# First attention of a two-layer block: the scaling of a pair's values on GpSimd instead of VectorE, its output product moved to the end of the step

## The reference, cut to what matters

```
x = x + attn0(layernorm(x))       # 16 heads of 64; q, k, v through 128x64 and 64x1024 weights
    scores = q @ k.T / 8          # 1024 x 1024 for each head and batch
    out = softmax(scores) @ v ; out @ fco_w + fco_b
x = x + ffn0(layernorm(x))        # 8 experts
    probs = softmax(logits); the two largest, divided by their sum, are the gates
    out = sum of gate * (silu(h1) * h2) @ down
x = x + attn1(layernorm(x)); x = x + ffn1(layernorm(x))
```

## Time and profile before

| | us |
|---|---|
| median of 3 runs | 1484.37 |
| lowest, highest run | 1483.67, 1501.54 |
| profiled execution: time | 1491.57 |
| its span | 1489.8 |
| its mean granted clock of TensorE | 0.967 |

### The profile page before, as it was taken

The page is one execution under the profiler, slowest core; times in us unless marked ns, Lnnn a source line. Parts: engine busy times, 40 slices in busy tenths (PEclk is TensorE's granted clock), DMA queues, the critical chain, the costliest instruction groups (busy, mean ns, idle before and its releaser), DMA issues. The chain is left out here.

```text
span 1489.8 us, 18635 instructions
## 1 busy us (share of the span) xinstructions
PE 1384.4 (93%) x6322; PEld 786.9 (53%) x6322; DVE 985.4 (66%) x1675; ACT 816.6 (55%) x1236; POOL 869.5 (58%) x685
## 2 busy tenths in 40 slices
PE   6699999999999999999988976899999997999998
PEld 5344445444544444444456733445444445687776
DVE  5677777777777767567546667676666724566665
ACT  4244444444444445444345444466776565787776
POOL 0298787778887867687654505455565332344443
PEclk9699999999999999999999997899999998999999
DMA  3110111111101111000040006011111106000000
GB/s 106 33 44 16 57 59 57 45 58 59 58 26 47 58 44 44 15 16 15 26 158 1 1 0 100 7 24 29 30 29 29 30 2 270 1 1 8 8 8 8
DMA packets 32586, 60.59 MB, mean 41 GB/s; under 512 B 9499, under 2 KB 17084, under 8 KB 32348
## 3 DMA queue, kind: packets, MB, share of 16 engines
q1 hardware_dynamic: 32492, 59.40, 14.4%
HBM read 35.13 MB, written 13.89 MB: 33 GB/s over the span
## 5 line engine op out<-in xcount | busy, mean ns | idle before, releaser
L628 POOL TENSOR_TENSOR psum_k<-psum_k,prob 128x1024 f32<-128x1024 f32 x186 | 464.3, 2519 | 78.7 <-ACT prob L680 78.7
L680 ACT ACTIVATE prob<-pair 128x1024 f32<-128x1024 f32 x256 | 249.4, 1025 | 388.7 <-PE pair L931 388.7
L738 DVE TENSOR_REDUCE mx<-pair 128x2 f32<-128x1024 f32 x256 | 303.9, 1221 | 83.5 <-PE pair L864 83.0
L903 PE MATMUL pv<-prob,c_all 128*64 128x512 f32 x1024 | 247.7, 605 | 0.0
L1928 DVE CUSTOM_DVE_ANT_0 l_banks<-l_banks,causal 128x128 f32<-128x128 f32 (+7 forms) x256 | 189.5, 783 | 74.3 <-PE l_banks L1966 73.3
L930 PE MATMUL pair<-qq,ak 128*128 128x512 f32 x512 | 221.5, 433 | 3.5 <-issue 2.4
L1836 ACT ACTIVATE l_prob<-l_banks 128x1024 f32<-128x1024 f32 (+7 forms) x256 | 155.2, 654 | 110.8 <-PE l_banks L1985 110.1
L931 PE MATMUL pair<-q,kb 128*128 128x512 f32 x512 | 202.3, 395 | 0.0
L2144 POOL TENSOR_TENSOR silu_rest_t<-silu_t,silu_lead_t 128x512 fp32r<-128x512 f32 x74 | 96.4, 1304 | 144.4 <-ACT silu_lead_t L2341 144.4
L1890 POOL TENSOR_SCALAR_AFFINE_SELECT l_prob<-l_prob 128x128 f32<-128x128 f32 x256 | 72.3, 295 | 146.2 <-ACT l_prob L1836 144.6
L930 PEld LDWEIGHTS pair<-qq,ak 128*128 128x128 f32 x512 | 97.0, 190 | 72.7 <-issue 35.2
(11 more groups left out here) (318 smaller groups left out, 2273.9 us busy)
## 6 DMA issues: line engine op xcount, KB each, us to landing
plain<-scratch_sums SPq DMA_DIRECT2D x32, 256.0 KB
whole<-in_experts SPq DMA_DIRECT2D x12, 512.0 KB, 5.1
scratch_lead<-rounded SPq DMA_DIRECT2D x12, 512.0 KB, 2.6
scratch_rest<-rounded SPq DMA_DIRECT2D x12, 512.0 KB, 3.9
w_lead_t<-scratch_lead SPq DMA_DIRECT2D x9, 512.0 KB, 6.4
w_rest_t<-scratch_rest SPq DMA_DIRECT2D x9, 512.0 KB, 7.3
l_kk<-rounded SPq DMA_DIRECT2D x16, 256.0 KB, 4.2
l_qq<-rounded SPq DMA_DIRECT2D x16, 256.0 KB, 5.4
```

The lines of the kernel that those rows point to most:

```text
L628: nc.gpsimd.tensor_tensor(total[:, h, :], total[:, h, :], prob[kt % 4][:, h, :], ALU.add).then_inc(summed, 1)
L680: nc.scalar.activation(prob[kt % 4][:, :, ts(j, BLK)], buffer("ST", at)[:, :, :], ACT.Exp, scale=D0 ** -0.5).then_inc(exp_done, 1)
L738: nc.vector.reduce_max(mx[:, x % 2, :, x // 2], buf[:, :, :], AX.X).then_inc(read, 1)
L903: ins = nc.tensor.matmul(pv[D0 * h:D0 * (h + 1), ts(j, BLK)], m.c_all[:, TT * (s // PAIRS) + kt, :], prob[kt % 4][:, h, ts(j, BLK)], start ...
```

## The change

Unit n (the scaling by the inverse sums) leaves VectorE. GpSimd does it between its half sums of key tiles 4 and 5, in every step but the first, after the inverse sums have landed (sums_moved), the values have been copied (ut_ready) and the output product of the pair before has read on (filled). The output product g moves from after the values of key tile 5 to the end of the step, after the values of key tile 6. In the gates' chain the probabilities get a function of their own; in the expert layer they stay in turn 10, the maxima move to turn 11 and the indices to turn 12.

```diff
--- before.py
+++ after.py
@@ -378,8 +378,8 @@
     5: [("s", 13), ("s", 14)],
 }
 AFTER_VALUES = {
-    0: [("s", 0)], 1: [("s", 3), ("l", 0)], 2: [("s", 6), ("X", 0)], 3: [("s", 9), ("r", 0)], 4: [("s", 12), ("n", 0)],
-    5: [("s", 15), ("g", 0)], 6: [("m", 0), ("R", 0), ("P", 0)],
+    0: [("s", 0)], 1: [("s", 3), ("l", 0)], 2: [("s", 6), ("X", 0)], 3: [("s", 9), ("r", 0)], 4: [("s", 12)],
+    5: [("s", 15)], 6: [("m", 0), ("n", 0), ("R", 0), ("P", 0)], 7: [("g", 0)],
 }
 
 
@@ -613,6 +613,12 @@
             for n in range(STEPS0):
                 total = psum_k[n % 2]
                 for kt in range(1, TT):
+                    if kt == TT - 3 and n:
+
+                        pool.wait_ge(sums_moved, 64 * n)
+                        pool.wait_ge(ut_ready, 2 * n)
+                        pool.wait_ge(filled, place(n - 1, ("g", 0)) + 1 if n > 1 else 1)
+                        nc.gpsimd.tensor_tensor(on[:, :], ut[:, :], rb[:, :], ALU.mult).then_inc(norm_done, 1)
                     for h in R2 if n < LAST else (0,):
 
                         pool.wait_ge(exp_done, 2 * TT * n + 2 * kt + 1 + 1)
@@ -769,10 +775,6 @@
                 elif kind == "r":
                     v.wait_ge(sums_moved, 64 * k + 16)
                     nc.vector.reciprocal(inv_c[:, :], sums_c[:, :]).then_inc(inv_ready, 1)
-                elif kind == "n":
-                    v.wait_ge(sums_moved, 64 * (k + 1))
-                    v.wait_ge(ut_ready, 2 * (k + 1))
-                    nc.vector.tensor_tensor(on[:, :], ut[:, :], rb[:, :], ALU.mult).then_inc(norm_done, 1)
                 else:
                     v.wait_ge(filled, u + 1)
                     out = m.out_t[:, ds(batch(k), T)]
@@ -793,7 +795,8 @@
             def run(units, base, done, ahead):
                 seen = 0
                 for kind, x in units:
-                    unit(kind, x, base + seen, done if kind in "lrng" else ahead)
+                    if kind != "n":
+                        unit(kind, x, base + seen, done if kind in "lrg" else ahead)
                     seen += kind not in "rn"
                     if ahead == AT_ROOT + 1 and kind == "s" and x in STATISTICS_BEHIND:
 
@@ -829,12 +832,14 @@
             seen = first_of(LAST)
             for what, *rest in step_script(LAST):
                 if what == "UNIT":
-                    unit(*rest, seen, LAST - 1)
+                    if rest[0] != "n":
+                        unit(*rest, seen, LAST - 1)
                     seen += rest[0] not in "rn"
                 elif what == "ST" and rest[1] and rest[0]:
                     add_last(rest[0])
                     if rest[0] == 1:
                         v.wait_ge(early_act, EXP)
+                        probabilities(nc, m, link)
                         choose_two(nc, m, link)
                     if rest[0] == 2:
                         index_two(nc, m, link)
@@ -998,13 +1003,17 @@
                             ALU.subtract).then_inc(shifted, 1)
 
 
-def choose_two(nc, m, link):
+def probabilities(nc, m, link):
 
     shape = [P, HALF, NEXP]
     link(nc.vector.reduce_sum(m.col[:, 1, :], m.ex[:, :, :], AX.X))
     link(nc.vector.reciprocal(m.col[:, 2, :], m.col[:, 1, :]))
     link(nc.vector.tensor_tensor(m.probs[:, :, :], m.ex[:, :, :], m.col[:, 2, :].unsqueeze(2).to_broadcast(shape),
                                  ALU.mult))
+
+
+def choose_two(nc, m, link):
+
     for t in range(HALF):
         ins = nc.vector.max(m.top[:, t, :], m.probs[:, t, :])
     link(ins)
@@ -1393,8 +1402,10 @@
                                  READ, gating)
                 elif n == 10:
                     v.wait_ge(tabled, EXP)
+                    probabilities(nc, m, link)
+                elif n == 11:
                     choose_two(nc, m, link)
-                elif n == 11:
+                elif n == 12:
                     index_two(nc, m, link)
                 elif n == 13:
                     write_gates(nc, m, link, 1, gating)
```

## The result

The changed kernel takes 1526.81 us, the median of four runs (1510.34, 1516.68, 1536.93, 1542.81), against 1488.43 us of the kernel before, measured beside it (1483.67 to 1501.54): slower, ratio 1.0166, 95% interval 1.0100 to 1.0232, so whether by 2% or more is unclear. The ratio is made from the two lower of the four runs, so it says nothing of the upper two. The profiled execution took 1510.34 us (span 1508.3). The forecast was 1495, with a range of 1477 to 1504.

The account below looks back on a forecast made before the run. TensorE's instruction list, busy for 93% of the span, was taken as the bound. From the median, 1484.37 + 16 (q late) - 0.6 (steps 12 to 14) - 4 (last step) = 1495.8; stated 1495 us, range 1477 to 1504.

Parts of the forecast that it names:

- GpSimd: one multiplication more a step: First attention, GpSimd's list: a multiplication of 2.36 us a step, list some 38 of 42.4 us, cost nothing by itself.
- q late by 1.45 us in eleven steps, +16: First attention, steps 1 to 11: remainders behind g's sum delay q, so score products wait; 1.45 us a step, +16 us.
- The two long stalls, -8.2: First attention: two stalls of about 4.1 us, where a GpSimd sum caught VectorE's scaling, go; -8.2 us in the profiled execution.
- The last step, -4: Last step of the first attention: TensorE no longer waits 2.84 us for the scaling and row sums start earlier; -4 us.
- The gates' chain, 0 (±2): Expert layer: a 3.39 us wait behind the indices goes, but TensorE then waits for a later product; 0 us, bounds ±2.
- The clock's rival: First attention: each wait between q and ST1 lowers TensorE's clock, 17 us on top, 1513 us; chance 0.10.
- The start from the median: Base of the sum: the runs' median, 7.2 us under the profiled execution, taken as nearly free of the two long stalls.
- the second rival: First attention: the runs of before have the long stalls too, so their 8.2 us leave the median as well; 1488 us, chance 0.15.

Follow-up runs that it names:

- e13: The changed kernel, nothing edited, measured a third time in a later series: 1530.06 us, ratio 1.0296 to the kernel before.
- e14: The changed kernel with mmax as a one-operand reduction, measured again in the series of e13: 1499.36 us, ratio 1.0074 to the kernel before.
- e16: The changed kernel with a small unused reduction before two-operand mmax and a GpSimd wait until mmax is done: 1496.85 us, ratio 1.0037 to the kernel before.
- e3: The changed kernel with the scaling back on VectorE at its old place, g still at the step's end: 1488.8 us, ratio 0.9983 to the kernel before.
- e2: The changed kernel with the weights' remainders run before g's sum instead of behind it: 1479.76 us, ratio 0.9937 to the kernel before.
- e6: The kernel before with a useless 128x1024 multiplication on GpSimd between its sums of key tiles 4 and 5: 1499.47 us, ratio 1.0073.
- e1: The changed kernel with mmax as a reduction over one SBUF operand instead of two: 1495.8 us, ratio 1.0040 to the kernel before.
- e9: The changed kernel, nothing edited, measured again in a later series: 1496.92 us, ratio 1.0052 to the kernel before.
- e10: The changed kernel with GpSimd waiting for two-operand mmax before its second half sum of key tile 5: 1495.42 us, ratio 1.0053 to the kernel before.
- e17: The changed kernel with one-operand mmax and the remainders before g's sum, measured again: 1486.67 us, ratio 0.9957 to the kernel before.
- e18: The kernel of e17 with the gates' chain as in the kernel before: 1481.13 us, ratio 0.9934 to the kernel before.
- e15: The changed kernel with a small unused reduction before two-operand mmax, in the series of e13: 1504.08 us, ratio 1.0088 to the kernel before.

## Why the prediction was wrong, point by point

**The step that failed** is "GpSimd: one multiplication more a step ... Cost: nothing by itself". I asked who waits for GpSimd and whether its list fills up, and both answers hold (2.43 us an instruction, row sums in time). I didn't ask who stands at the port while it has no rest. The runs show mmax there: 8.24 us beside the row in e13 and the first profile, gone with one operand (e14) and with a rest for GpSimd (e16). The multiplication fills the gaps of 0.31 and 1.61 us of the earlier trace rows, in which VectorE's two-operand instructions used to get in. In the first profile that cost three times 8 us in mmax. It is +25.0 over before, where these three steps had 3 x 1.45 = 4.4 in the sum. I did count contention, for the remainders alone, and as at most one GpSimd instruction's length at a time. The rule of the Trainium skill, "SBUF — State Buffer", Who interferes with whom, says that a VectorE instruction with two SBUF inputs and a GpSimd one that reads SBUF exclude each other. By this rule, the traces agree: 8.24 us with two inputs, 0.19 us with one. But whoever comes next isn't whoever waited, as the 8.24 us of a 0.18 us instruction show.

That it takes the multiplication to make the row long enough is read from the timelines and not shown by a run. Before, four half sums also follow each other without a rest, and the remainders asked for in them take 2.9 us at most; the version without the multiplication (e3) ran in a series in which nothing was starved with it either (e2), and e6, which adds one to the kernel before, delays the scaling but no mmax.

**q late by 1.45 us in eleven steps, +16.** Right in mechanism and near in size: the idle time of 2.98 us is gone, q's wait is 0.87 us, the step is 43.7 us where I said 43.9. It stood in eight steps of the first profile (two of them starved ones), not eleven: behind each of the three starved mmax GpSimd has rested, the pair of remainders takes about 2 us instead of 4.17, and q is in time. In e1, with nothing starved, it stands in all eleven. Removing it (e2) gives the whole of it back.

**The two long stalls, -8.2.** Gone: -8.8. e3 shows them tied to the scaling on VectorE.

**The last step, -4.** Measured -4.3. **The gates' chain, 0 (±2).** +1.2 in the profile. **The clock's rival** (gaps like q's taking it): not so; waits of 0.87 us left the plain step at 43.7, while the clock averaged 0.62 behind one of 5.78 us.

**The start from the median.** I took the runs of before to be free of the long stalls, since they were 7 us under the profiled one. With some 30 runs beside e9 the kernel before has a median of 1490.03 and a spread of 1482.74 to 1503.07, so that assumption is not supported, and the second rival's premise has something in it. The changed kernel with nothing starved, at 1495.4 to 1499.4 (e1, e9, e10, e14, e16), does come near the 1495 forecast, but by an increase of 5 to 9 us over the medians beside it rather than 11, from a start that lay too low: that agreement is in part luck. The profile of e9 has the same: from the first q product to the expert layer it takes 719.9 us against 721.0 before, so in these two executions q's waits cost about what the long stalls and the last step give back, and the rest of the difference lies behind the middle (735.8 us against 732.3), for which I have no cause beyond the gates' chain.

**What stays open.** What lets mmax in at the first boundary in most steps and keeps it out at three in others, at instants equal to within 0.03 us; and why one chip or launch starves four steps and another none. The upper runs (1536.93, 1542.81, 1562.98) would fit six to ten starved steps, by my estimate, at 6.4 to 7.6 us each over the 1495 of none, but they weren't profiled, and the 1514 to 1534 of e17 and e18 show that a one-operand mmax doesn't keep such runs away.

## What to carry to other kernels

Before filling the idle gaps of GpSimd, list VectorE's instructions with two SBUF operands that are asked for during its row: each may have to wait for the end of the row, not of one instruction. Where one is on the path, write it with a single SBUF operand (e1, e14), or give GpSimd a wait at that place, which cost nothing measurable here (e10 beside e9, e16 beside e15). Then run it in several series: a single one may show no long wait at all (e2, e9). And when a unit moves to the end of a step, look at what stands behind all units: the remainders, not g, made q late.

## What was not expected of the hardware

A VectorE instruction of 128x16 with two SBUF operands, 0.18 us alone, lasted 8.24 us beside four more GpSimd instructions of 2.3 us each; with one operand it lasted 0.19 us beside the same row. The same program ran at 1492 to 1506 us in one series (e9) and at 1523 to 1563 in another (e13), while the median of the kernel before was equal in both (1490.03 and 1490.13).
